# A MoE kernel's second part: pairs of blocks by turns with shared or with routed experts first

## The chip, the cores and the metric

One core of a Trainium2 chip runs the kernel; nothing else runs on the chip. The metric is the time of one execution on the device in microseconds (us); the time of the kernel before is the median of its executions.

## What is computed

Tokens x are 32 samples of 128 tokens of 128 features. Two layers of the same shape are applied, x = x + ffn(cond(x)) twice. In the first, cond is a mixture of 4 experts chosen 2 per sample, and ffn one of 8 experts that all run. The change lies in the second layer:

```
def _L1_cond_ref(x, t_emb, W_router, router_bias, s_w1, s_w3, s_w2, r_w1, r_w2):
    ...
    for e in range(N_SHARED):                      # 2 shared experts
        h = jax.nn.silu(x_flat @ s_w1[e].T) * (x_flat @ s_w3[e].T)
        shared_out = shared_out + h @ s_w2[e].T
    ...
    s = jax.nn.sigmoid((router_in @ W_router.T).astype(jnp.float32))
    _, topk_idx = jax.lax.top_k(s + router_bias, 2)
    ...                                            # gates: s of the two chosen, over their sum
    for e in range(N_EXPERTS):                     # 8 routed experts
        h = jax.nn.gelu(x_flat @ r_w1[e].T, approximate=False)
        routed_out = routed_out + h @ r_w2[e].T * gates_full[:, e:e + 1]
    out = (shared_out + routed_out) / (N_SHARED + TOP_K)

def _L1_ffn_ref(x, U1, V1, b1, U2, V2, b2):        # low rank, 32
    P = x @ U1;  H = jax.nn.gelu(P @ V1 + b1);  Q = H @ U2
    return Q @ V2 + b2
```

## The kernel before

The 4096 tokens are 8 blocks of 512 columns (NBLK, BLK), features on the 128 partitions. Work is a list of items, made by plan(): A and G are the first layer's mixture, B its ffn, and the second layer has S (shared expert, 4 items a block), R (routed expert, 8 items a block, one per expert) and F (final low-rank layer, 4 items a block). An item's number in the list is its slot; every engine's program is a loop over the slots, so the list orders all of them.

An item goes through the engines like this. TensorE's up() makes its columns in one of four PSUM banks (NZ, zb), three matmuls for each result since every fp32 number is split in a high and a low part (XHL; the weights WCH, WCL). S has two results, R and F one, and F's up is one matmul. ScalarE applies Silu (S, line 999), Gelu (R, line 995) or the tanh Gelu (F, line 992), each from another function table, so that an ACT_TABLE_LOAD stands where the kind changes. VectorE multiplies into Hf: for S the second result (line 1442), for R the token's gate for this expert (line 1449). Then the result is split again: HH, the high part, on ScalarE (line 1005) or VectorE (1459), HL, the rest, on VectorE (1462) or GpSimd (1542). The assignment is by kind: for R, HH is VectorE's for one item in four and HL is VectorE's for one in four; for S, HL is VectorE's but for blocks 2 and 3, where GpSimd has it. Five slots behind the up (LAG) comes down(), two matmuls from HH and HL (lines 897, 899) that add to one of two PSUM banks (ob), which a block holds from its first S or R item to its last.

The gates lie in the tile CWB, in 8 places of 128 x 512, one per expert; SyncE loads a place from the scratch tensor in HBM, a row spread over 128 partitions, 256 KB, for the next block as soon as the block before has multiplied by it (gate_slots, line 617). The gates themselves come from the choice, which is made twice: choose(0, .) for blocks 0 to 3 and choose(1, .) for blocks 4 to 7. Each is a sigmoid on ScalarE (line 959), some two dozen small VectorE operations spread over ten slots (pick; lines 1258 to 1310), a transposition on TensorE (line 808) and a write to scratch by SyncE.

When a block's S and R items are all down, low_rank (lines 965 and 1419) makes PS, from which F's ups start; behind F come read_q (970, 1427), last_mm (823) and add_y (1434), and the output leaves.

The order of the second part: for each pair of blocks b, b+1 the 8 S items, then F of the pair before, then the 16 R items. F of block 4 stands in the last pair, F of 5, 6 and 7 at the end (LATE).

Of the kernel before, what the change touches and what calls it, by code (L numbers as in the profile page):

```python
# [23 lines left out]
NO = 2  # L24
# [101 lines left out]
def build(nc, x_d, small_d, pack_d, wa_d, wb_d, wc_d, wf_d, scr_d, wup_d, wdown_d, out_d):  # L126
    with ExitStack() as ctx:
# [125 lines left out]
        def done(kind, blk, ex, f):  # L253
            return pos[kind, blk, ex, f].d
# [4 lines left out]
        t_c = [done("R", b, 7, 0) for b in range(NBLK)]  # L259
# [14 lines left out]
        for t, g in soft_a.items():  # L274
            for step, slot in ((0, 0), (2, 2), (3, 2), (4, 3), (5, 3)) if g == 0 else ((0, 0), (2, 2), (3, 3), (4, 4), (5, 5)):
# [4 lines left out]
                [pos["S", 2, 0, 0].k + i for i in (0, 1, 2, 3, 4, 5, 6, 7, 9, 10)]]  # L280
# [548 lines left out]
        def up(e, it):  # L829
            for j, z in enumerate(it.z):  # L830
# [12 lines left out]
                fresh = it.f == 0 and j == 0 and it.ex == 0  # L843
# [17 lines left out]
                if fresh and it.kind == "S":  # L861
                    e.wait_ge(s_b_hi, it.blk + 1)
# [17 lines left out]
                if fresh and it.kind == "S":  # L880
                    e.wait_ge(s_b_lo, it.blk + 1)
# [39 lines left out]
        def scalar_program(e):  # L921
# [11 lines left out]
            for k in range(slots):  # L933
# [26 lines left out]
                if k in low_rank:  # L960
                    b = low_rank[k]
                    e.wait_ge(s_down, pos["R", b, 7, 0].n + 1)
                    if ph_free(("P", b)):
                        e.wait_ge(*ph_free(("P", b)))
                    e.activation(PH[:, :], ob[pos["R", b, 7, 0].u % NO][:, :], ACT.Copy).then_inc(s_ph, 1)
# [46 lines left out]
        def vector_program(e):  # L1012
# [336 lines left out]
            for k in range(slots):  # L1349
# [303 lines left out]
```

## Time and profile before

| | us |
|---|---|
| median of 3 runs | 901.16 |
| lowest and highest | 900.01, 903.05 |
| the profiled execution | 900.65 |
| its span, first to last instruction | 898.9 |
| TensorE busy | 875.0 |
| VectorE busy | 683.0 |
| ScalarE busy | 576.9 |
| GpSimd busy | 408.7 |

The time has 1.75 us around the span. The granted TensorE clock is 0.997 of full speed over the span. Matmuls are pipelined, so that TensorE's busy time covers short stalls; its starts tell more. The second layer's part runs from about 725 us to the end.

### The profile page before, as it was taken

Reading aid. Unit: us, or ns where it says so; the run is one execution under the profiler, and the core shown is the slowest. Engines: PE = TensorE matmul, PEld = TensorE weight load, DVE = VectorE, ACT = ScalarE, POOL = GpSimd, SP = SyncE. Lnnn points to the kernel's source line nnn. Section 1 sums busy time; section 2 is a strip of 40 time slices with the busy share of each in tenths; the row PEclk is TensorE's granted clock in tenths of the full one; section 3 lists DMA queues with packets and bytes.
Section 4 is the critical chain, followed back from the end, with each engine's and each line's share of the span. In section 5 each row is a group of like instructions: output and inputs, shape, how many; then the busy total and the mean of one; then the engine's idle time right before and its main releaser. Section 6 shows DMA issues by size and latency. Waiting matters only on the chain.

```text
span 898.9 us, 12685 instructions
## 1 busy us (share of the span) xinstructions
PE 875.0 (97%) x3878; PEld 694.6 (77%) x3878; DVE 683.0 (76%) x1097; ACT 576.9 (64%) x1032; POOL 408.7 (45%) x378
## 2 busy tenths in 40 slices
PE   8899999999999999999999999999999998999996
PEld 5778788878888888888888888888888785777773
DVE  7667777878789786686686686686666876998887
ACT  7788788765555455555555555555555677989896
POOL 7447865035256352252253253253222226755465
PEclk9999999999999999999999999999999999999999
DMA  9588882023023112012012012011010069182640
GB/s 311 195 251 273 297 285 100 1 85 132 13 82 109 36 47 82 1 47 82 1 48 82 1 48 82 1 47 48 7 42 1 0 107 175 39 179 52 159 106 35
DMA packets 35828, 82.96 MB, mean 92 GB/s; under 512 B 4400, under 2 KB 14256, under 8 KB 33840
## 3 DMA queue, kind: packets, MB, share of 16 engines
q1 hardware_dynamic: 35760, 82.15, 30.8%
q8 instruction: 31, 0.51, 0.3%
q14 instruction: 37, 0.30, 0.1%
HBM read 71.13 MB, written 6.83 MB: 87 GB/s over the span
## 4 chain that ended last, share of the span: by engine, by line
PE 77%; DVE 8%; issue 4%; ACT 3%; DMA 3%; SPq 2%; POOL 2%; POOLq 0%; DVEq 0%; ACTq 0%
PE ps L863 17%; PE ps L882 16%; PE ps L868 16%; PE ps L917 8%; PE ps L919 8%; PE ps L912 8%; DMA CWB<-scratch 2%; DVE HL L1462 2%; PE ps L899 1%; PE ps L897 1%; ACT HH L1005 1%; DVE HH L1459 1%; POOL HL L1542 1%; DVE Hf L1449 1%; SPq L722 1%
## 5 line engine op out<-in xcount | busy, mean ns | idle before, releaser
L999 ACT ACTIVATE Sg<-ps 128x512 f32<-128x512 f32 x288 | 171.8, 598 | 246.2 <-PE ps L882 245.8
L1442 DVE TENSOR_TENSOR Hf<-ps,Sg 128x512 f32<-128x512 f32 x288 | 198.0, 688 | 149.1 <-ACT Sg L999 93.2
L1542 POOL TENSOR_TENSOR HL<-Hf,HH 128x512 fp32r<-128x512 f32 x136 | 182.3, 1347 | 172.4 <-ACT HH L1005 154.6
L1005 ACT ACTIVATE HH<-Hf 128x512 fp32r<-128x512 f32 x346 | 216.2, 625 | 24.9 <-DVE Hf L1442 12.9
L1462 DVE TENSOR_TENSOR HL<-Hf,HH 128x512 fp32r<-128x512 f32 x242 | 214.7, 887 | 4.2 <-ACT HH L1005 3.2
L863 PE MATMUL ps<-XHL,WBH 128*128 128x512 f32 x512 | 203.7, 398 | 1.2 <-DVE Hf L1442 1.2
L882 PE MATMUL ps<-XHL,WBH 128*128 128x512 f32 x512 | 202.1, 395 | 0.0
L868 PE MATMUL ps<-XHL,WBL 128*128 128x512 f32 x512 | 202.0, 395 | 0.0
L1557 POOL TENSOR_TENSOR XT<-XT,TMP 128x512 f32<-128x512 f32 x64 | 84.2, 1316 | 251.5 <-DVE TMP L1338 251.5
L863 PEld LDWEIGHTS ps<-XHL,WBH 128*128 128x128 f32 x512 | 96.1, 188 | 25.1 <-DVE Hf L1442 2.3
L882 PEld LDWEIGHTS ps<-XHL,WBH 128*128 128x128 f32 x512 | 96.0, 188 | 23.1
L868 PEld LDWEIGHTS ps<-XHL,WBL 128*128 128x128 f32 x512 | 96.2, 188 | 21.8
L1462 DVE TENSOR_TENSOR HL<-ps,HH 128x512 fp32r<-128x512 f32 (+1 forms) x122 | 73.7, 618 | 37.6 <-ACT HH L1005 36.4
L917 PE MATMUL ps<-HH,WBL 128*128 128x512 f32 x256 | 101.1, 395 | 0.0
L912 PE MATMUL ps<-HH,WBH 128*128 128x512 f32 x256 | 100.8, 394 | 0.0
L919 PE MATMUL ps<-HL,WBH 128*128 128x512 f32 x256 | 100.7, 393 | 0.0
L992 ACT ACTIVATE ps<-ps,GWU 128x512 f32<-128x512 f32 (+1 forms) x84 | 48.8, 585 | 17.8 <-PE ps L882 17.4
L917 PEld LDWEIGHTS ps<-HH,WBL 128*128 128x128 f32 x256 | 48.0, 188 | 11.9
L912 PEld LDWEIGHTS ps<-HH,WBH 128*128 128x128 f32 x256 | 48.0, 187 | 11.9 <-DVE TMP L1338 0.3
L919 PEld LDWEIGHTS ps<-HL,WBH 128*128 128x128 f32 x256 | 48.1, 188 | 11.2
L863 PE MATMUL ps<-XHL,WCH 128*128 128x512 f32 x128 | 51.9, 405 | 3.7 <-DVE Hf L1449 2.4
L1449 DVE TENSOR_TENSOR Hf<-ps,CWB 128x512 f32<-128x512 f32 x64 | 42.8, 682 | 10.4 <-ACT ps L995 7.9
(254 smaller groups left out, 1347.3 us busy)
## 6 DMA issues: line engine op xcount, KB each, us to landing
CWB<-scratch SPq DMA_DIRECT2D x68, 256.0 KB, 7.9
CWB<-scratch SPq DMA_DIRECT2D x15, 1024.0 KB, 4.7
GWD<-expert_down SPq DMA_DIRECT2D x21, 576.5 KB, 4.6
GWU<-expert_up SPq DMA_DIRECT2D x21, 514.0 KB, 5.1
ST<-in_wb_dram SPq DMA_DIRECT2D x8, 768.0 KB, 6.3
GX<-XT SPq DMA_DIRECT2D x68, 64.0 KB, 2.8
XT<-in_x_dram SPq DMA_DIRECT2D x8, 256.0 KB, 5.3
expert_up<-GWU SPq DMA_DIRECT2D x4, 512.0 KB, 3.8
```

What stands on the lines that cost most here:

```text
L863: e.matmul(o, wh, tokens(it, 0), start=True, stop=False)
L868: e.matmul(o, wl, tokens(it, 0), start=False, stop=False)
L882: e.matmul(o, wh, tokens(it, 1), start=False, stop=True).then_inc(s_z, 1)
L912: e.matmul(bk[:, 0:n], wh, HH[:, hs, 0:n], start=it.new, stop=False)
L917: e.matmul(bk[:, 0:n], wl, HH[:, hs, 0:n], start=False, stop=False)
L919: e.matmul(bk[:, 0:n], wh, HL[:, hs, 0:n], start=False, stop=it.last).then_inc(s_down, 1)
L999: e.activation(Sg[:, it.n % NG, :], zb[z % NZ][:, :], ACT.Silu).then_inc(s_act, 1)
L1005: e.activation(HH[:, it.n % NH, 0:it.cols], hidden_place(it), ACT.Copy).then_inc(s_hi_act, 1)
L1442: e.tensor_tensor(Hf[:, it.n % NS, :], zb[z % NZ][:, :], Sg[:, it.n % NG, :], ALU.mult).then_inc(s_prod, 1)
L1462: e.tensor_tensor(l, f, h.bitcast(F32), ALU.subtract).then_inc(s_lo_dve, 1)
L1542: e.tensor_tensor(HL[:, it.n % NH, :], Hf[:, it.n % NS, :], HH[:, it.n % NH, :].bitcast(F32), ALU.subtract).then_inc(s_lo_pool, 1)
L1557: e.tensor_tensor(XT[:, it.blk, :], XT[:, it.blk, :], TMP[:, t % 2, :], ALU.add).then_inc(s_acc, 1)
```

## The change

For pairs 0 and 2 (blocks 0, 1, 4, 5) S comes first and R last, for pairs 1 and 3 (blocks 2, 3, 6, 7) R first and S last. F of the pair before stands between the two in every pair, as it did. The mark of a block's last item is set where the list ends it, R for the one kind of pair and S for the other, and what went by R's eighth item (t_c, the bank, the semaphore's count) goes by that item. TensorE's waits for a block's tokens are at the block's first item, S or R. The second choice starts at the same slot as before, 24 items behind the second part's start, where R2 stands now and S2 stood.

```
 S0 S1 R0 R1  S2 S3 F0 F1 R2 R3  S4 S5 F2 F3 R4 R5  S6 S7 F4 R6 R7  F5 F6 F7   before
 S0 S1 R0 R1  R2 R3 F0 F1 S2 S3  S4 S5 F2 F3 R4 R5  R6 R7 F4 S6 S7  F5 F6 F7   after
```

```
--- before.py
+++ after.py
@@ -103,17 +103,21 @@
         return [Item("S", blk, f // 2, f % 2, False) for f in range(4)]
 
     def routed(blk):
-        return [Item("R", blk, e, 0, e == 7) for e in range(8)]
+        return [Item("R", blk, e, 0, False) for e in range(8)]
 
     def final(blk):
         return [Item("F", blk, 0, f, f == 3) for f in range(4)]
 
+
     for b in range(0, NBLK, 2):
-        items += shared(b) + shared(b + 1)
+        one, two = (shared, routed) if b % 4 == 0 else (routed, shared)
+        items += one(b) + one(b + 1)
         for f in (b - 2, b - 1):
             if 0 <= f < LATE:
                 items += final(f)
-        items += routed(b) + routed(b + 1)
+        for c in (b, b + 1):
+            items += two(c)
+            items[-1].last = True
     for b in range(LATE, NBLK):
         items += final(b)
     return items
@@ -256,7 +260,8 @@
         t_g = done("G", NGRP - 1, 0, 3)
         t_a = [max(t_g, done("A", b, 0, 3)) for b in range(NBLK)]
         t_b = [done("B", b, 7, 3) for b in range(NBLK)]
-        t_c = [done("R", b, 7, 0) for b in range(NBLK)]
+        end_c = [next(it for it in real if it.kind in "SR" and it.blk == b and it.last) for b in range(NBLK)]
+        t_c = [it.d for it in end_c]
         t_f = [done("F", b, 0, 3) for b in range(NBLK)]
 
         def when(times, after=0):
@@ -277,7 +282,7 @@
         exp_a = {t + 1: g for t, g in soft_a.items()}
 
         pick = [[lag_b[3] + 1 + i for i in (0, 1, 2, 3, 5, 6, 7, 8, 10, 11)],
-                [pos["S", 2, 0, 0].k + i for i in (0, 1, 2, 3, 4, 5, 6, 7, 9, 10)]]
+                [pos["R", 2, 0, 0].k + i for i in (0, 1, 2, 3, 4, 5, 6, 7, 9, 10)]]
         pick_at = {}
         for g in range(2):
             for i, t in enumerate(pick[g]):
@@ -840,7 +845,7 @@
                     continue
                 o = zb[z % NZ][:, 0:it.cols]
                 wh, wl = up_weights(it, j)
-                fresh = it.f == 0 and j == 0 and it.ex == 0
+                fresh = it.new and j == 0 if it.kind in "SR" else it.f == 0 and j == 0 and it.ex == 0
                 if it.kind == "A" and it.blk == 0 and it.f == 0:
                     e.wait_ge(s_wa_hi, 1)
                 if it.kind == "G" and it.f == 0:
@@ -858,7 +863,7 @@
                         e.wait_ge(s_x_end, 2 * it.blk - 11)
                 if fresh and it.kind == "B":
                     e.wait_ge(s_a_hi, it.blk + 1)
-                if fresh and it.kind == "S":
+                if fresh and it.kind in "SR":
                     e.wait_ge(s_b_hi, it.blk + 1)
                 e.matmul(o, wh, tokens(it, 0), start=True, stop=False)
                 if it.kind == "A" and it.blk == 0 and it.f == 0:
@@ -877,7 +882,7 @@
                     e.wait_ge(s_g_lo, it.blk + 1)
                 if fresh and it.kind == "B":
                     e.wait_ge(s_a_lo, it.blk + 1)
-                if fresh and it.kind == "S":
+                if fresh and it.kind in "SR":
                     e.wait_ge(s_b_lo, it.blk + 1)
                 e.matmul(o, wh, tokens(it, 1), start=False, stop=True).then_inc(s_z, 1)
 
@@ -959,10 +964,10 @@
                     e.activation(pick_place(g)[0], LR[:, 16 * g:16 * g + 16, 0:8], ACT.Sigmoid).then_inc(s_exp, 1)
                 if k in low_rank:
                     b = low_rank[k]
-                    e.wait_ge(s_down, pos["R", b, 7, 0].n + 1)
+                    e.wait_ge(s_down, end_c[b].n + 1)
                     if ph_free(("P", b)):
                         e.wait_ge(*ph_free(("P", b)))
-                    e.activation(PH[:, :], ob[pos["R", b, 7, 0].u % NO][:, :], ACT.Copy).then_inc(s_ph, 1)
+                    e.activation(PH[:, :], ob[end_c[b].u % NO][:, :], ACT.Copy).then_inc(s_ph, 1)
                 if k in read_q:
                     b = read_q[k]
                     e.wait_ge(s_down, pos["F", b, 0, 3].n + 1)
@@ -1417,7 +1422,7 @@
                     if b >= 2:
                         e.wait_ge(s_z, pos["F", b - 2, 0, 3].z[0] + 1)
                     e.scalar_tensor_tensor(out=PS[:, b % 2, :], in0=PH[:, :].bitcast(F32), scalar=col("m2"),
-                                           in1=ob[pos["R", b, 7, 0].u % NO][:, :], op0=ALU.mult,
+                                           in1=ob[end_c[b].u % NO][:, :], op0=ALU.mult,
                                            op1=ALU.add).then_inc(s_ps, 1)
                 if k in read_q:
                     b = read_q[k]
```

VectorE, from the last multiplications of R1 to the second choice's first six operations, first before, then after (the number behind L is the line; in the changed kernel lines are 5 higher):

```order
L1449 TENSOR_TENSOR Hf<-ps,CWB 128x512
L1442 TENSOR_TENSOR Hf<-ps,Sg 128x512
L1459 CAST HH<-Hf 128x512
L1258 TENSOR_TENSOR ps<-ps,sm 128x128
L1260 TENSOR_REDUCE r<-ps 128x16
L1262 TENSOR_TENSOR ps<-ps,r 128x128
L1442 TENSOR_TENSOR Hf<-ps,Sg 128x512
L1265 TENSOR_TENSOR ps<-ps,sm 128x128
L1267 TENSOR_REDUCE r<-ps 128x16
L1269 TENSOR_TENSOR q<-ps,r 128x128
L1442 TENSOR_TENSOR Hf<-ps,Sg 128x512
```

```order
L1454 TENSOR_TENSOR Hf<-ps,CWB 128x512 x2
L1464 CAST HH<-Hf 128x512
L1263 TENSOR_TENSOR ps<-ps,sm 128x128
L1265 TENSOR_REDUCE r<-ps 128x16
L1267 TENSOR_TENSOR ps<-ps,r 128x128
L1454 TENSOR_TENSOR Hf<-ps,CWB 128x512
L1270 TENSOR_TENSOR ps<-ps,sm 128x128
L1272 TENSOR_REDUCE r<-ps 128x16
L1274 TENSOR_TENSOR q<-ps,r 128x128
L1454 TENSOR_TENSOR Hf<-ps,CWB 128x512
L1467 TENSOR_TENSOR HL<-Hf,HH 128x512
```

The eight S multiplications (L1442) beside the choice's small operations give place to R's (L1454), with VectorE's HL (L1467) and HH (L1464) of R between them. The low-rank operation of block 1, which stands behind the fourth step in both, isn't shown.

ScalarE at the same place, before and after:

```order
L995 ACTIVATE ps<-ps 128x512
L1005 ACTIVATE HH<-Hf 128x512
L959 ACT_TABLE_LOAD
L959 ACTIVATE ps<-LR 128x128
L999 ACT_TABLE_LOAD
L999 ACTIVATE Sg<-ps 128x512 x2
L1005 ACTIVATE HH<-Hf 128x512
L999 ACTIVATE Sg<-ps 128x512
```

```order
L1000 ACTIVATE ps<-ps 128x512
L1010 ACTIVATE HH<-Hf 128x512
L964 ACT_TABLE_LOAD
L964 ACTIVATE ps<-LR 128x128
L1000 ACT_TABLE_LOAD
L1000 ACTIVATE ps<-ps 128x512 x2
L1010 ACTIVATE HH<-Hf 128x512
L1000 ACTIVATE ps<-ps 128x512
```

The sigmoid stays between two table loads; the second loads R's table where it loaded S's.

SyncE, from the write of the first choice to the end, before and after:

```order
L684 DMA scratch<-q 128x128
L617 DMA CWB<-scratch 128x512 x24
L684 DMA scratch<-q 128x128
L617 DMA CWB<-scratch 128x512 x6
L699 DMA out_dram<-CB 128x512
L617 DMA CWB<-scratch 128x512 x4
L699 DMA out_dram<-CB 128x512
L617 DMA CWB<-scratch 128x512 x12
L699 DMA out_dram<-CB 128x512
```

```order
L689 DMA scratch<-q 128x128
L622 DMA CWB<-scratch 128x512 x32
L689 DMA scratch<-q 128x128
L622 DMA CWB<-scratch 128x512 x8
L704 DMA out_dram<-CB 128x512 x2
L622 DMA CWB<-scratch 128x512 x6
L704 DMA out_dram<-CB 128x512
L622 DMA CWB<-scratch 128x512 x4
L704 DMA out_dram<-CB 128x512
```

Loads of gates (L617, now L622) come 32 in a row instead of 24 ahead of the second choice's write (L684, now L689), and the outputs of blocks 0 and 1 (L699, now L704) leave behind the loads for block 4 instead of among those for block 3 and block 4.

## Rows read from the trace of the kernel before

**Rows 1.** The page's first part: busy us, share of the span, instructions.

```profile
PE 875.0 (97%) x3878; PEld 694.6 (77%) x3878; DVE 683.0 (76%) x1097; ACT 576.9 (64%) x1032; POOL 408.7 (45%) x378
```

**Rows 2.** Windows: PE, PEld, DVE, ACT, POOL busy us, TensorE clock, DMA share, GB/s.

```profile
731.70:754.60 22.90, 20.88 (x85) 15.19 (x84) 15.20 (x26) 16.15 (x30) 12.80 (x10) 1.00 0.99 178
754.60:780.00 25.40, 22.90 (x95) 16.95 (x94) 20.90 (x44) 22.15 (x35) 17.69 (x13) 1.00 0.36 62
780.00:798.40 18.40, 18.40 (x79) 13.96 (x77) 17.74 (x28) 16.53 (x32) 14.60 (x12) 1.00 0.83 185
798.40:822.30 23.90, 22.30 (x92) 16.61 (x91) 19.69 (x29) 20.73 (x33) 6.88 (x5) 1.00 0.33 58
822.30:840.40 18.10, 18.10 (x80) 14.66 (x79) 17.79 (x29) 16.20 (x32) 14.78 (x12) 1.00 0.76 179
...
860.30:878.10 17.80, 17.40 (x72) 12.66 (x71) 16.89 (x25) 15.92 (x32) 14.56 (x12) 1.00 0.54 134
878.10:898.90 20.80, 12.83 (x44) 7.13 (x42) 15.90 (x25) 11.96 (x20) 10.21 (x8) 0.95 0.10 38
```

**Rows 3.** The tile CWB, 725.7 to 758.3: ns min/median/max, first and last start us.

```profile
L617 SPq DMA_DIRECT2D CWB<-scratch x24: 320/1412/1844, 725.7 to 756.6; - x24
L1449 DVE TENSOR_TENSOR Hf<-ps,CWB x16: 678/692/693, 731.7 to 754.6; 128x512 f32<-128x512 f32 x16
...
DMA to landing us min/median/max: 3.8/9.9/11.3
```

**Rows 4.** VectorE's timeline: start us, us, engine, line, operation, tiles, idle before.

```profile
735.60 0.69 DVE L1449 TENSOR_TENSOR Hf<-ps,CWB 128x512 f32<-128x512 f32 x1 [0.26 <-DMA CWB<-scratch]
...
753.18 0.69 DVE L1449 TENSOR_TENSOR Hf<-ps,CWB 128x512 f32<-128x512 f32 x1 [0.38 <-issue]
```

**Rows 5.** The chain of waits, 741 to 756 us: start, us, what.

```profile
743.07 9.74 DMA CWB<-scratch
```

**Rows 6.** ScalarE's timeline at the second choice's sigmoid.

```profile
754.55 1.28 ACT L959 ACT_TABLE_LOAD   x1
...
756.15 1.28 ACT L999 ACT_TABLE_LOAD   x1
757.44 1.09 ACT L999 ACTIVATE Sg<-ps 128x512 f32<-128x512 f32 x2
```

**Rows 7.** VectorE's timeline, steps of the second choice.

```profile
758.68 0.42 DVE L1459 CAST HH<-Hf 128x512 fp32r<-128x512 f32 x1
759.01 0.29 DVE L1258 TENSOR_TENSOR ps<-ps,sm 128x128 f32<-128x128 f32 x1
...
759.87 0.68 DVE L1442 TENSOR_TENSOR Hf<-ps,Sg 128x512 f32<-128x512 f32 x1
760.47 0.29 DVE L1265 TENSOR_TENSOR ps<-ps,sm 128x128 f32<-128x128 f32 x1
...
768.11 1.18 DVE L1301 TENSOR_SCALAR r<-r 128x16 f32<-128x16 f32 x1
```

**Rows 8.** Line 1442: S multiplications of blocks 2-3, 4-5 and 6-7.

```profile
L1442 DVE TENSOR_TENSOR Hf<-ps,Sg x8: 666/680/692, 758.1 to 770.1; 128x512 f32<-128x512 f32 x8
...
L1442 DVE TENSOR_TENSOR Hf<-ps,Sg x8: 676/687/692, 800.2 to 811.4; 128x512 f32<-128x512 f32 x8
...
L1442 DVE TENSOR_TENSOR Hf<-ps,Sg x8: 679/688/692, 842.1 to 853.3; 128x512 f32<-128x512 f32 x8
```

**Rows 9.** TensorE's timeline, one S item.

```profile
725.63 0.39 PE L863 MATMUL ps<-XHL,WCH 128*128 128x512 f32 x1
...
727.48 0.39 PE L863 MATMUL ps<-XHL,WCH 128*128 128x512 f32 x1
```

**Rows 10.** The tile CWB, 822.2 to 841, blocks 4 and 5.

```profile
L1449 DVE TENSOR_TENSOR Hf<-ps,CWB x16: 673/677/692, 822.3 to 840.4; 128x512 f32<-128x512 f32 x16
L617 SPq DMA_DIRECT2D CWB<-scratch x15: 319/320/1837, 823.0 to 839.1; - x15
...
DMA to landing us min/median/max: 3.0/6.7/10.7
```

More of the change, by code:

```diff
@@ L105, in routed @@
     def routed(blk):
-        return [Item("R", blk, e, 0, e == 7) for e in range(8)]
+        return [Item("R", blk, e, 0, False) for e in range(8)]
     def final(blk):
@@ L111, in plan @@
     for b in range(0, NBLK, 2):
-        items += shared(b) + shared(b + 1)
+        one, two = (shared, routed) if b % 4 == 0 else (routed, shared)
+        items += one(b) + one(b + 1)
         for f in (b - 2, b - 1):
@@ L115, in plan @@
                 items += final(f)
-        items += routed(b) + routed(b + 1)
+        for c in (b, b + 1):
+            items += two(c)
+            items[-1].last = True
     for b in range(LATE, NBLK):
@@ L258, in build @@
         t_b = [done("B", b, 7, 3) for b in range(NBLK)]
-        t_c = [done("R", b, 7, 0) for b in range(NBLK)]
+        end_c = [next(it for it in real if it.kind in "SR" and it.blk == b and it.last) for b in range(NBLK)]
+        t_c = [it.d for it in end_c]
         t_f = [done("F", b, 0, 3) for b in range(NBLK)]
@@ L279, in build @@
         pick = [[lag_b[3] + 1 + i for i in (0, 1, 2, 3, 5, 6, 7, 8, 10, 11)],
-                [pos["S", 2, 0, 0].k + i for i in (0, 1, 2, 3, 4, 5, 6, 7, 9, 10)]]
+                [pos["R", 2, 0, 0].k + i for i in (0, 1, 2, 3, 4, 5, 6, 7, 9, 10)]]
         pick_at = {}
@@ L842, in up @@
                 wh, wl = up_weights(it, j)
-                fresh = it.f == 0 and j == 0 and it.ex == 0
+                fresh = it.new and j == 0 if it.kind in "SR" else it.f == 0 and j == 0 and it.ex == 0
                 if it.kind == "A" and it.blk == 0 and it.f == 0:
@@ L860, in up @@
                     e.wait_ge(s_a_hi, it.blk + 1)
-                if fresh and it.kind == "S":
+                if fresh and it.kind in "SR":
                     e.wait_ge(s_b_hi, it.blk + 1)
@@ L879, in up @@
                     e.wait_ge(s_a_lo, it.blk + 1)
-                if fresh and it.kind == "S":
+                if fresh and it.kind in "SR":
                     e.wait_ge(s_b_lo, it.blk + 1)
@@ L961, in scalar_program @@
                     b = low_rank[k]
[L962 removed]
+                    e.wait_ge(s_down, end_c[b].n + 1)
                     if ph_free(("P", b)):
                         e.wait_ge(*ph_free(("P", b)))
[L965 removed]
+                    e.activation(PH[:, :], ob[end_c[b].u % NO][:, :], ACT.Copy).then_inc(s_ph, 1)
                 if k in read_q:
```

2 lines of the change are left out of this document (1 added, 1 removed).

## The prediction

> **What bounds the kernel now.** I read the page's first part, then the second part of the program stretch by stretch (the windows), then the one tile that the new order uses more densely (CWB, the gates), then the timelines of VectorE and ScalarE around the choice. S2 is the shared experts of block 2, R2 its routed experts (R2.0 to R2.7, one item each), F2 its final layer; blocks count from 0, so the third block is block 2.
>
> TensorE is busy 97% of the span [rows 1], so a gain must come from where it waits. Up to the routed experts of blocks 0 and 1 both programs have the same instructions in the same order on every engine; the change lies after 731.7 us, in the last 167 us. There it is busy 18.4 of 18.4 us beside R2 and R3 and 18.1 of 18.1 beside R4 and R5, but 20.9 of 22.9 beside R0 and R1, 22.9 of 25.4 beside S2, S3, F0, F1, and 12.8 of 20.8 in the tail [rows 2]. So two pairs of routed blocks run without a loss and one pair does not, with the same arithmetic in each. The DMA column tells them apart: 0.99 beside R0 and R1, 0.83 and 0.76 beside the others. Every routed item multiplies by a gate row that was spread over 128 partitions, 256 KB, and there are 8 places for such rows, one per expert. The place is loaded again only after the block before has used it. R0 and R1 run back to back on loads that have just begun: 24 loads follow each other, 9.9 us from issue to landing in the median and up to 11.3, and even the issue takes SyncE 1.4 us in the median against 0.32 at the least [rows 3]. VectorE is released by such a load at 735.60 (R0.3) and, by the chain of waits, again at 753.18 (R1.6) [rows 4, 5]. Between them lie 11 loads: 17.58 / 11 = 1.60 us for a load, while an item needs about 1.2 us of the compute engines (18.1 us from first to last of 16, over 15 intervals). R2 to R5 escape this because in the order of before every second block's loads arrive during 24 items of S and F.
>
> **What the change does to that, part by part.** I count on VectorE's clock: the start of the multiplication that ends each stage, since TensorE, which runs at most four results ahead of it, ends up behind the same event.
>
> *R0 and R1*: unchanged, last multiplication at 754.6.
>
> *R2 and R3 now follow at once.* Their 16 loads are not hidden any more. R3.7 is 17 loads behind R1.6: 753.18 + 17 x 1.60 = 780.4. Against this stands what VectorE has to do. The sigmoid of the second choice stays between two table loads of 1.28 us [rows 6], so R2.0 is multiplied at 758.1 as S2.0 is now. The choice took 12.0 us from 758.1 to 770.1 beside eight S multiplications [rows 7, 8]: three dependent steps of 0.33 us a slot (759.01 to 759.87) and one slot with a step of 1.18 us. In those slots of before GpSimd computes HL for S; for R VectorE has two of the eight HL (0.6 us from start to start) and two HH (0.34) besides, so R2.7 comes at 770.1 + 1.2 + 0.3 = 771.6. Eight more items at 0.9 (VectorE alone: 0.6 for the multiplication, a quarter of 0.6 and of 0.34, and the copy) to 1.16 us (five matmuls of 0.232 [rows 9]) end between 778.8 and 780.9. Loads and choice thus end about together; neither is added to the other, since the loads already queued go on landing while VectorE chooses. I take 780.2 for R3.7. Bounds: 778.7, if a load takes 1.50; 784, if the choice's delay also delays the reissue of loads by its full 4 us.
>
> *F0 and F1* then cost what they cost behind S3 now: from S3's last multiplication at 770.1 to R2.0 at 780.0, 9.9 us [rows 2, 8], two table loads in it either way: 790.1.
>
> *S2 to S5 in a row.* Sixteen items, 15 intervals. One S item is eight matmuls, 725.63 to 727.48 = 1.85 us [rows 9], and TensorE is the slowest engine there. Eight of them took 11.2 us instead of 7 x 1.85 = 13.0, since TensorE enters ahead; that 1.8 is had once: 15 x 1.85 - 1.8 = 26.0, so 816.1. The outputs of F0 and F1 move from R2 and R3 to here, where VectorE has room; I cost them at nothing, and 0.7 us each if they hadn't.
>
> *F2 and F3*: as now, 811.4 to 822.3 = 10.9 [rows 2, 8]: R4.0 at 827.0.
>
> *R4 to R7 in a row.* R4's loads are long in. R5's first load is issued 0.7 us after R4.0's multiplication (823.0 against 822.3) and lands 3.0 later, then latency climbs to 10.7 because loads at 1.6 follow items at 1.2 [rows 10]. With two blocks in a row the climb ends before it hurts; with four, 24 loads queue: 0.7 + 3.0 + 23 x 1.60 = 40.5 us from R4.0 to R7.7, against 18.1 + 1.2 + 17.8 = 37.1 when the loads are in time. So 867.5.
>
> *F4*, now behind R7: as now behind S7, 853.3 to 860.3 = 7.0: 874.5. *S6 and S7*: 11.2: 885.7. *The tail*, F5 to F7 with the outputs: 898.9 - 878.1 = 20.8: 906.5.
>
> *What goes.* Sigmoid to S2, R3 to S4 and R5 to S6 are three joins that vanish, F to S and R to F come in their place; the table loads of the second part fall, by the two programs' order, from 12 to 10, 2 x 1.28 = 2.6 us of ScalarE. This is already in the sum, since I went from stage to stage; ScalarE is at 16.2 to 16.5 of 18.1 to 18.4 us beside R and not the bound [rows 2].
>
> Sum: 906.5 - 898.9 = +7.6 us. The profiled execution took 900.65, so 908.2 for its like; the median of the runs is 901.16, 0.5 above, so **908.8**.
>
> Two rules would have it otherwise. The Trainium skill, ScalarE: Activation LUTs, Table sets: the hidden batching unit and the rules behind it, says to do all work of one table set before switching, at about 2.66 us for each switch (What ACT_TABLE_LOAD costs); that speaks for the change and would make its two fewer switches worth 5.3 us. The trace has 1.28 us for a load, and the next activation starts 0.02 us behind it [rows 6]. The Trainium skill, DMA: Bandwidth & Descriptors, Anatomy of one DMA, fits a transfer at 2.0 us plus its bytes over 436e3 (for transfers issued by GpSimd), which is an estimate of 0.6 us a load for 256 KB when several overlap; then no routed item would ever wait for a gate. The trace has 1.60, with all 16 DMA engines at a share of 0.99.
>
> **The rivals.**
>
> *A. The sum above*: gates bound eight blocks' worth in two long runs. For it: the two pairs of before differ in nothing but the state of the loads.
>
> *B. The loads keep up, and fewer switches pay.* If the 1.60 were not a rate of the DMA engines but came from the start (R0's eight loads issued at once) then loads at the pace of the items would land in time. R3.7 would come at 754.6 + 3.5 (sigmoid) + 18.4 = 776.5 or so, 3.7 earlier, and R4 to R7 would take 37.1, 3.4 less: +0.5 us; with one table load of 1.28 and the join R3 to S4 (1.8 us from 798.4 to 800.2, of which 0.6 is the wait of the table) gained, 900 to 902. It decides if a load lands faster than one in 1.2 us. For it: bytes moved are only 178 GB/s. Against it: the share of 0.99, and that beside R4 and R5, issued one by one, latency climbs from 3.0 to 10.7 as well.
>
> *C. The choice does not fit beside R2.* TensorE has to transpose the choice's result two slots behind it, in front of its own item, and all that is queued behind (the ups of R3, the downs of R2) waits for VectorE. If VectorE's extra work in these slots (about 7 us of choice, 12.0 less eight times 0.6) is paid after the loads instead of under them, R3.7 comes at 784: 912.6.
>
> *D. A load takes 1.50.* In the two drains the last loads may come closer. Then R0 to R3 end 1.5 earlier, R4 to R7 2.3 earlier, and the F stretches behind R, whose table load needn't wait for an HH of ScalarE, are each 0.4 shorter: 904.2.
>
> **How the numbers follow.** A 0.52, D 0.22, C 0.12, B 0.14. A measurement here tells 0.3% (2.7 us) from nothing. A, C and D are slower than 903.9, D in most of its width; B is half faster, half the same. Slower 0.84, same 0.09, faster 0.07. The range 903.5 to 912.5 leaves out B and half of C.
>
> **What would show it.** The multiplications by gates: 32 in a row with R3.7 near 780, DMA share near 1.0 from 731 to 780 and from about 840 to 867, TensorE waiting for VectorE's L1454 (L1449 now) and VectorE for the landing of CWB in R2, R3 and R7. S2 to S5 at 1.85 us an item without a wait. No wait for CWB in R2 and a DMA share under 0.9 would mean B; VectorE busy without a gap from 758 to 780 with loads landed well before use would mean C. I am wrong if R4 to R7 take 37 us.

## The result, and the profile after

The changed kernel takes 912.46 us (median of 4 runs, 911.04 to 914.89), against 901.07 for the kernel before beside it. The ratio is 1.0129 [1.0114, 1.0143], 11.6 us of 901. The forecast was 908.8, range 903.5 to 912.5: slower, as said, but 11.6 us where 7.6 were forecast. By the ratio on 901.16 us the time is 912.8 (901.16 x 1.0129), just above the range. The profiled execution took 912.01 us with a span of 910.2. VectorE's multiplication by a gate is L1454, that of an S item L1447, TensorE's transposition of the choice L813, the choice's last step L1312.

The first part of the page of the changed kernel, as [rows 1]:

```profile
PE 878.5 (97%) x3878; PEld 697.4 (77%) x3878; DVE 682.9 (75%) x1097; ACT 574.6 (63%) x1030; POOL 407.4 (45%) x378
```

Work is the same on every engine but ScalarE, which has two instructions less. So the 11.6 us are waiting, and work at a lower clock. The windows show where; columns as in [rows 2] (busy us of PE, PEld, DVE, ACT, POOL, then clock, DMA share, GB/s). In order: R0 and R1; R2 and R3; F0 and F1; S2 to S5; F2 and F3; R4 and R5; R6 and R7 with their start; F4 with S6 and S7; the tail.

```profile
731.30:753.80 22.50, 20.89 (x85) 15.21 (x85) 15.03 (x26) 15.91 (x29) 12.80 (x10) 1.00 1.02 182
753.80:783.30 29.50, 21.75 (x77) 15.77 (x76) 21.26 (x51) 19.16 (x34) 15.41 (x13) 0.88 0.81 145
783.30:794.20 10.90, 9.24 (x36) 6.06 (x35) 9.77 (x12) 9.47 (x15) 6.50 (x5) 1.00 0.69 135
794.20:820.70 26.50, 26.50 (x116) 21.42 (x116) 18.00 (x27) 18.98 (x35) 11.59 (x9) 1.00 0.06 21
820.70:831.60 10.90, 9.71 (x39) 6.70 (x38) 9.13 (x11) 10.83 (x17) 4.35 (x3) 1.00 0.01 2
831.60:849.70 18.10, 18.10 (x80) 14.71 (x79) 17.78 (x29) 16.23 (x32) 14.66 (x12) 1.00 0.78 183
849.70:871.00 21.30, 19.66 (x80) 14.15 (x79) 16.31 (x27) 15.97 (x30) 16.04 (x13) 1.00 0.77 165
871.00:888.00 17.00, 16.80 (x71) 12.55 (x70) 14.70 (x22) 14.06 (x24) 5.43 (x4) 1.00 0.01 1
888.00:910.20 22.20, 14.18 (x52) 8.73 (x50) 16.52 (x27) 13.40 (x23) 7.69 (x6) 0.91 0.13 47
```

Two rows matter. Beside R2 and R3, TensorE works 21.75 of 29.5 us and its granted clock is 0.88; in [rows 2] no pair of R takes over 22.9 and every window in front of the tail has a clock of 1.00. Beside R6 and R7 it works 19.66 of 21.3 us, where a pair with its loads in time is busy 18.1 of 18.1.

Put against the terms of the prediction, from one last multiplication on VectorE to the next (us):

| stretch | predicted | after | off |
|---|---|---|---|
| start to R1.7 | 754.6 | 753.8 | -0.8 |
| R1.7 to R3.7 | 25.6 | 29.5 | +3.9 |
| F0, F1, to S2.0 | 9.9 | 10.9 | +1.0 |
| S2 to S5 | 26.0 | 26.5 | +0.5 |
| F2, F3, to R4.0 | 10.9 | 10.9 | 0 |
| R4 to R7 | 40.5 | 39.3 | -1.2 |
| F4, to S6.0 | 7.0 | 6.0 | -1.0 |
| S6, S7 | 11.2 | 11.1 | -0.1 |
| tail | 20.8 | 22.2 | +1.4 |

The sum is 910.2 instead of 906.5. One stretch carries the miss, R1.7 to R3.7. The first row is no finding: up to R1.7 the programs are the same, and the traces with 256 KB loads have R1.7 anywhere from 753.2 to 754.8. VectorE's timeline there, at R2.3, at the end of the choice with R2.7, and at R3.7 (start, us, line, operation, idle time before):

```profile
764.53 0.69 DVE L1454 TENSOR_TENSOR Hf<-ps,CWB 128x512 f32<-128x512 f32 x1 [1.66 <-DMA CWB<-scratch]
...
771.92 0.37 DVE L1312 TENSOR_TENSOR q<-ps,q 128x128 f32<-128x128 f32 x1
772.15 1.26 DVE L1454 TENSOR_TENSOR Hf<-ps,CWB 128x512 f32<-128x512 f32 x2
...
783.27 0.68 DVE L1454 TENSOR_TENSOR Hf<-ps,CWB 128x512 f32<-128x512 f32 x1
```

And TensorE's:

```profile
768.44 0.50 PE L904 MATMUL ps<-HL,WD 128*128 128x512 f32 x1 [0.52 <-POOL HL L1547]
...
772.44 0.30 PE L813 MATMUL ps<-sm,q 128*128 128x128 f32 x1 [3.50 <-DVE q L1312]
772.50 0.48 PE L868 MATMUL ps<-XHL,WCH 128*128 128x512 f32 x1
...
773.35 0.63 PE L902 MATMUL ps<-HH,WD 128*128 128x512 f32 x1
773.77 0.63 PE L904 MATMUL ps<-HL,WD 128*128 128x512 f32 x1
774.20 0.63 PE L868 MATMUL ps<-XHL,WCH 128*128 128x512 f32 x1
```

VectorE waits for a gate once, 1.66 us at R2.3, and never again up to R3.7. TensorE instead stands for 3.50 us in front of the transposition L813, which needs the choice's last step. Behind it in its queue are the ups of R3 and the downs of R2, and they come in a burst when it ends. From 773.35 on matmuls start 0.42 to 0.43 us apart, where [rows 9] has 0.23 (1.85 us for eight). Three short windows of the same columns, the last two inside slow spells, the first in front of one:

```profile
753.80:758.00 4.20, 2.38 (x11) 1.58 (x9) 1.21 (x3) 4.08 (x6) 1.30 (x1) 1.00 1.08 154
...
760.00:762.00 2.00, 2.00 (x5) 1.61 (x6) 1.93 (x6) 1.66 (x4) 1.11 (x1) 0.50 0.69 128
...
774.00:776.00 2.00, 2.00 (x6) 1.52 (x6) 0.89 (x2) 0.99 (x3) 2.00 (x2) 0.50 1.00 175
```

A clock of 0.50 is the lower of TensorE's two levels, 1.2 instead of 2.4 GHz. It is granted twice, 759.5 to 762.9 and 773.2 to 776.6, 3.4 us each. Ahead of the first TensorE was busy 2.38 of 4.2 us (the join around the sigmoid of the second choice), ahead of the second it did nothing from 770 to 772 (the transposition). What decides between the levels is not shown: the same 4.2 us behind R1.7 in the kernel before have TensorE busy 2.54 us, and its clock stays at 1.00 there, and behind it too [rows 2]:

```profile
754.60:758.80 4.20, 2.54 (x10) 1.34 (x8) 1.43 (x4) 3.89 (x6) 1.28 (x1) 1.00 1.02 163
```

By an estimate, half of 6.8 us, 3.4 us of matmul time, is lost if TensorE is the bound throughout.

The loads of that stretch (tile CWB, 725 to 758; columns of [rows 3]):

```profile
L622 SPq DMA_DIRECT2D CWB<-scratch x24: 320/1441/1836, 725.1 to 755.5; - x24
...
DMA to landing us min/median/max: 3.8/10.6/14.6
```

They are those of [rows 3] but for one that took 14.6 us, the one R2.3 waited for. While it was under way, a 16 KB packet of the queue that brings instructions took 6.1 us; no packet of such a queue took over 2.4 us in the other traces. R2.7 came 18.3 us behind R1.7 here, and 16.3 and 16.4 us in two kernels below without a late load (no reload; the transposition later). So some 2 us of R2 in this execution belong to one load. The median of the runs is no lower than this execution, though; where the other executions lost as much isn't shown. A kernel below that turns only blocks 2 and 3 has the same program up to here and no late load in its trace: its R1.7 to R3.7 is 27.9 us.

### The profile page after: what moved, and what is told of

Its sections match the earlier page's. It is cut to its first block, busy times and chain, and to the rows that moved or that the text cites. A ratio compares the mean times of both kernels' runs of the same rounds, so it can differ in the third digit from the quotient of the medians.

```text
span 910.2 us, 12683 instructions
## 1 busy us (share of the span) xinstructions
PE 878.5 (97%) x3878; PEld 697.4 (77%) x3878; DVE 682.9 (75%) x1097; ACT 574.6 (63%) x1030; POOL 407.4 (45%) x378
## 4 chain that ended last, share of the span: by engine, by line
PE 75%; DVE 8%; DMA 7%; issue 4%; ACT 3%; SPq 2%; POOL 1%; POOLq 0%; DVEq 0%; ACTq 0%
PE ps L868 16%; PE ps L887 16%; PE ps L873 16%; PE ps L922 8%; PE ps L924 8%; PE ps L917 8%; DMA CWB<-scratch 6%; DVE HL L1467 2%; PE ps L904 1%; ACT HH L1010 1%; PE ps L902 1%; DVE HH L1464 1%; DVE Hf L1454 1%; PE ps L790 1%; DMA XT<-in_x_dram 1%
## 5 line engine op out<-in xcount | busy, mean ns | idle before, releaser
L1447 DVE TENSOR_TENSOR Hf<-ps,Sg 128x512 f32<-128x512 f32 x288 | 198.1, 689 | 150.3 <-ACT Sg L1004 88.7
L1467 DVE TENSOR_TENSOR HL<-Hf,HH 128x512 fp32r<-128x512 f32 x242 | 211.2, 873 | 4.0 <-ACT HH L1010 3.2
L873 PEld LDWEIGHTS ps<-XHL,WBL 128*128 128x128 f32 x512 | 96.2, 188 | 21.7
L1467 DVE TENSOR_TENSOR HL<-ps,HH 128x512 fp32r<-128x512 f32 (+1 forms) x122 | 73.7, 618 | 36.4 <-ACT HH L1010 35.3
L1454 DVE TENSOR_TENSOR Hf<-ps,CWB 128x512 f32<-128x512 f32 x64 | 43.4, 685 | 21.7 <-ACT ps L1000 10.9
L922 PEld LDWEIGHTS ps<-HH,WBL 128*128 128x128 f32 x256 | 48.0, 188 | 11.8
L924 PEld LDWEIGHTS ps<-HL,WBH 128*128 128x128 f32 x256 | 48.1, 188 | 11.2
```

Source lines behind the costliest of these rows:

```text
L873: e.matmul(o, wl, tokens(it, 0), start=False, stop=False)
L922: e.matmul(bk[:, 0:n], wl, HH[:, hs, 0:n], start=False, stop=False)
L924: e.matmul(bk[:, 0:n], wh, HL[:, hs, 0:n], start=False, stop=it.last).then_inc(s_down, 1)
L1447: e.tensor_tensor(Hf[:, it.n % NS, :], zb[z % NZ][:, :], Sg[:, it.n % NG, :], ALU.mult).then_inc(s_prod, 1)
L1467: e.tensor_tensor(l, f, h.bitcast(F32), ALU.subtract).then_inc(s_lo_dve, 1)
```

## The experiments

All results are ratios to the kernel before, run beside each kernel, with a 95% interval; it ran at 899.8 to 900.3 us there, about 1 us below the 901.07 above, so a time in us compares with one of the first runs only after that 1 us. Stages are from one trace of each kernel, on VectorE's multiplications, as in the table. A *join* is the time from the last multiplication of one stretch to the first of the next. For comparison, in the kernel before: R0 to R1 22.9, S2 to S3 12.0, R2 to R3 18.4, R4 to R5 18.1, tail 20.8.

### The choice back beside S2

```
-                [pos["R", 2, 0, 0].k + i for i in (0, 1, 2, 3, 4, 5, 6, 7, 9, 10)]]
+                [pos["S", 2, 0, 0].k + i for i in (0, 1, 2, 3, 4, 5, 6, 7, 9, 10)]]
...
         def pick_place(g):
-            if g:
-                return [v(ab_bank("pick")[:, i * 128:i * 128 + 128]) for i in range(3)]
             return v(q2[:, 0:128]), v(q2[:, 128:256]), v(q3[:, 128:256])
```

> The changed order, with the second choice begun 24 items later, beside S2 instead of R2, its three intermediate arrays in SBUF (as the first choice has them) instead of a PSUM bank. In the changed kernel the multiplications went from R1.7 to R3.7 in 29.5 us, with TensorE waiting 3.8 us for the choice's result ahead of its transposition, and the clock granted at half twice for 3.4 us. Theory 1 (the choice beside R2 is what made this stretch longer than the loads' 25.6): it falls to 25 to 26, the half clock is gone, and S2, S3 take it without a loss; 907.5 to 909.5 us in all. Theory 2 (the loads alone bound the stretch, and the late load of R2.3 of that one execution did the rest): 911.5 to 913, and the stretch stays above 28.

Measured 912.42, 1.0141 [1.0122, 1.0160], where neither theory holds as written: the stretch fell below what the first said, and the whole didn't fall at all. R1.7 to R3.7 fell from 29.5 to 22.3 (join 0.6, R2 and R3 21.7) with no wait in front of a transposition and no half clock there. But F0, F1 to S2.0 came to 12.6, and S2 and S3 took 18.1 instead of 12.0. The window of S2 and S3, and VectorE and GpSimd in it:

```profile
789.30:807.40 18.10, 14.29 (x57) 10.27 (x57) 17.62 (x34) 9.84 (x18) 10.47 (x8) 1.00 0.04 16
```

```profile
789.86 1.40 DVE L1257 TENSOR_TENSOR q<-q,sm 128x128 f32<-128x128 f32 x1
791.29 0.29 DVE L1259 TENSOR_REDUCE r<-q 128x16 f32<-128x128 f32 x1
791.62 1.11 DVE L1261 TENSOR_TENSOR q<-q,r 128x128 f32<-128x128 f32 x1
```

```profile
789.81 1.30 POOL L1541 TENSOR_TENSOR HL<-Hf,HH 128x512 fp32r<-128x512 f32 x1 [3.34 <-ACT HH L1004]
791.31 1.27 POOL L1541 TENSOR_TENSOR HL<-Hf,HH 128x512 fp32r<-128x512 f32 x1 [0.20 <-ACT HH L1004]
```

The edit did more than move the choice. It had no PSUM bank there, so its arrays lie in SBUF, and a step that takes 0.29 us with an operand in PSUM [rows 7] takes 1.40 while GpSimd runs its 1.30 us subtraction, and 1.11 beside the next. The Trainium skill, SBUF — State Buffer, SBUF: two separate sides, has the rule: a port pair is shared by VectorE and GpSimd as an exclusive lock, taken for a whole instruction, and a VectorE operation with two SBUF inputs needs it against a GpSimd operation that reads SBUF. By that rule, the trace agrees: the 1.40 us step ends just behind GpSimd's instruction, the reduction with one input is at 0.29. So this run shows that R1.7 to R3.7 is 7.2 us shorter without the choice beside it, some 2 of them by the late load, but not what the move would bring in all.

### No loads of gates after the first block of a half

```
-            for ex in range(8):
+            for ex in range(8 if b % 4 == 0 else 0):
...
-                    e.wait_ge(f_gate[it.ex], 16 * (it.blk + 1))
+                    e.wait_ge(f_gate[it.ex], 16 * (it.blk // 4 + 1))
```

> The changed kernel without the reloads of gates: blocks 1 to 3 multiply by block 0's gates, 5 to 7 by block 4's, so 16 loads of 256 KB are left of 64. Theory 1 (choice bounds R2 and R3, loads bound R0, R1 and R4 to R7): R0 and R1 take 19 to 20 instead of 22.6 us, R4 to R7 37 instead of 39.3, R2 and R3 still 27 to 28 instead of 29.5; 905 to 907.5 us. Theory 2 (loads bound all of it): R2 and R3 fall to about 22, and the whole to 899 to 902.

The same on the kernel before:

> The kernel before without the reloads of gates (blocks 1 to 3 multiply by block 0's, 5 to 7 by block 4's). Only R0 and R1 wait for loads in it: their 22.9 us fall to 19 or 20, and the whole to 897 to 898.5. The difference to the changed kernel without reloads is then what order and choice cost without any load.

| | ratio | R0 to R1 | R1.7 to R3.7 | R6 to R7 |
|---|---|---|---|---|
| after | 1.0129 | 22.5 | 29.5 | 21.3 with its join |
| after, no reload | 1.0057 [1.0040, 1.0074] | 19.1 | 28.1 | 18.8 with its join |
| before, no reload | 0.9968 [0.9957, 0.9979] | 19.1 | | |

The first theory holds for the changed kernel (905.21 us), and the second run is within what it expected once it is put on 901 us (898.2). The loads cost the new order 1.0129 - 1.0057 = 0.0072, 6.5 us, and the old one 2.9. But R2 and R3, the stretch that I had bound by loads, gain 1.4 us of their 29.5 when the loads are gone. The waits of the run without them, its multiplications, and its window of half clock:

```profile
PE ps L813 <- DVE q L1312: 3.5, 1, 3.5
```

```profile
L1454 DVE TENSOR_TENSOR Hf<-ps,CWB x16: 672/680/692, 754.0 to 778.8; 128x512 f32<-128x512 f32 x16
```

```profile
765.40:772.20 6.80, 4.99 (x13) 3.96 (x14) 4.38 (x12) 3.42 (x7) 3.84 (x3) 0.50 0.04 11
```

The wait of 3.5 us at the transposition is there with no reload at all, and so is the half clock, 6.8 us in one piece. Here it is not granted behind the join R1 to R2 but from 765.1 on, while TensorE still stands in front of the transposition.

### No second choice, with and without the loads

The second choice is left out, and blocks 4 to 7 are gated by the first one's scratch. Three kernels: after without the choice; after without choice and reloads; before without both.

```
-        for g in range(2):
+        for g in range(1):
             for i, t in enumerate(pick[g]):
...
-                    e.wait_ge(f_scr[1][b // 4], 16)
-                    src = scr_d[1, b // 4].rearrange("(e t) k -> e (t k)", e=8)[ex][
+                    e.wait_ge(f_scr[1][0], 16)
+                    src = scr_d[1, 0].rearrange("(e t) k -> e (t k)", e=8)[ex][
```

> The changed kernel without the second choice (no sigmoid, no choice on VectorE, no transposition): blocks 4 to 7 multiply by the gates of blocks 0 to 3, loaded as before. By the stages seen: R1 to R3.7 at the loads' pace, 22 to 23 us instead of 29.5, the rest as in the changed kernel: 904 to 906 us. That would put the choice's cost in this order at 6 to 8 us. If the choice cost only the wait at the transposition (3.5 us), it is 908 to 909.

> The changed order without the second choice and without reloads of gates (blocks 1 to 7 multiply by block 0's gates, loaded twice). What is left is the order of S, R and F. Stages: 19.6 + 0.6 + 18.2 for R0 to R3, 10.9, 26.5 for S2 to S5, 10.9, 36.9, 6.0, 11.1, 22.2: 895 to 897 us.

> The kernel before without the second choice and without reloads, as the mate of the last one. Kernel before without reloads is 897.0; the join R1 to S2 falls from 3.4 to 1.8 and S2, S3 from 12.0 to 11.1: 893 to 895 us. If order alone is neutral, both are level; by my stages this one is 1.5 to 2.5 us faster, from the tail behind R7 (20.7) against S7 (22.2) and the join R3 to F0 (10.9 against 9.9).

Measured 904.46, 1.0042 [1.0026, 1.0059]; 896.56, 0.9960 [0.9946, 0.9975]; and 894.75, 0.9934 [0.9918, 0.9951]: all three within 1 us of what was expected. With the runs above this makes a table of four for R1.7 to R3.7 in the new order:

| | no loads | loads |
|---|---|---|
| no choice | 18.9 | 22.1 |
| choice | 28.1 | 29.5 |

Loads alone, from the kernel after without the choice (tile CWB, then the window):

```profile
L1452 DVE TENSOR_TENSOR Hf<-ps,CWB x17: 683/691/693, 753.6 to 775.7; 128x512 f32<-128x512 f32 x17
...
DMA to landing us min/median/max: 5.2/9.5/10.7
```

```profile
753.60:775.70 22.10, 20.07 (x78) 13.53 (x77) 15.40 (x27) 15.56 (x30) 15.36 (x12) 1.00 1.01 197
...
762.00:765.00 3.00, 2.51 (x11) 1.60 (x10) 2.31 (x5) 2.23 (x5) 2.26 (x2) 1.00 0.97 305
```

That is a stretch bound by loads: DMA share 1.01, 16 intervals in 22.1 us, so 1.38 us a load. It isn't the 1.60 of the run from R0.3 to R1.6. Nor is it an even pace: the landings of the stretch are 0.6 to 2.4 us apart, and in the 3 us of the second row 305 GB/s move at nearly the same DMA share. So a load had no fixed price here, and 1.60 and 1.38 are averages.

With the choice the stretch is 29.5, and loads add 1.4 to 28.1 instead of 3.2 to 18.9, with the late load among the 1.4. In the trace without a late load (only blocks 2 and 3 turned, below) it is 27.9 with all its loads, no longer than without any: they do hide under the choice.

With the two orders each run with both, without loads and without either, the parts of the whole have a price (as a share of the kernel before's time, and in us):

| | old order | new order | difference |
|---|---|---|---|
| neither | 0.9934 | 0.9960 | 0.0026, 2.3 us |
| choice adds | 0.0034 | 0.0097 | 0.0063, 5.7 us |
| loads add to that | 0.0032 | 0.0072 | 0.0040, 3.6 us |

The sum of the differences is 11.6 us, as it must be; each difference is good to 2 or 3 us, since each ratio has an interval of 0.001 to 0.002 to either side. So about half of the loss is the choice beside R2. The order alone, without either, also loses: every one of its 5 runs (896.35 to 898.20) is above the 4 of the old order (894.18 to 895.57). About 1.5 us of it is the tail, 22.2 against 20.8 in their traces.

### The transposition four slots later

```
-                [pos["R", 2, 0, 0].k + i for i in (0, 1, 2, 3, 4, 5, 6, 7, 9, 10)]]
+                [pos["R", 2, 0, 0].k + i for i in (0, 1, 2, 3, 4, 5, 6, 7, 13, 14)]]
```

> The changed kernel with the second choice's transposition on TensorE four items later (R3.5 instead of R3.1), and the copy behind it. It takes the in-order wait in front of R3.1 away and leaves the choice's work on VectorE where it is. If that wait (3.8 us of TensorE, and the half clock after it) is on the path: R2.7 to R3.7 falls from 11.1 to 8 or 9 us and the whole to 909 to 910.5. If VectorE itself is the bound there: no change, 912 to 913.

Measured 908.94, 1.0098 [1.0081, 1.0115]. No instruction is removed; TensorE's transposition only stands four items further back, and the copy of its result with it. Its wait is gone, so is the second spell of half clock, and R1.7 to R3.7 is 25.8 (join 3.5, then 22.3) instead of 29.5, of which some 2 us are the late load. R2.7 to R3.7 takes 9.4 instead of 11.1 (11.8 without reloads). Of the whole this is worth 1.0129 - 1.0098 = 0.0031, 3 us, good to 2. The multiplications and the window:

```profile
L1454 DVE TENSOR_TENSOR Hf<-ps,CWB x16: 670/680/692, 758.3 to 780.6; 128x512 f32<-128x512 f32 x16
```

```profile
758.30:781.00 22.70, 19.23 (x70) 13.49 (x70) 21.91 (x49) 15.70 (x29) 15.31 (x12) 0.92 0.58 133
```

VectorE is busy 21.91 of 22.70 us: this is the case that I had forecast, where VectorE's work sets the end, and the stretch takes the 25.6 us of the forecast to 0.2. One spell of half clock is left, 3.4 us at 760.4.

### One pair at a time

The rule of the order with one pair turned, blocks 2 and 3 or blocks 6 and 7 (the latter with the choice beside S2, where the old order has it):

```
-        one, two = (shared, routed) if b % 4 == 0 else (routed, shared)
+        one, two = (shared, routed) if b != 2 else (routed, shared)
```

> One half of the change: only blocks 2 and 3 have R first (R2 R3 F0 F1 S2 S3), blocks 6 and 7 have S first as before. By the stages of both traces, added up, this half has 9.3 of the 11.3 us: 909.5 to 911. If the two halves depend on each other (ScalarE's two fewer table loads, the outputs), it would differ from 901.1 + 9.3 by over 2 us.

> The other half of the change: only blocks 6 and 7 have R first (R6 R7 F4 S6 S7), blocks 2 and 3 have S first and the second choice stands beside S2 as before. By the stages: R4 to R7 39.3 us instead of 18.1 + 17.8 and the joins between, F4 and tail: +2.0 us, so 902.5 to 904. If the loads cost nothing in it, it ends at 900 to 901.5.

Measured 908.77, 1.0104 [1.0087, 1.0121] and 902.09, 1.0020 [1.0009, 1.0031]; 9.4 and 1.8 us, 11.2 together of 11.6, so within the noise of some 2 us the two pairs don't act on each other. Turning blocks 6 and 7 gives R6 and R7 at 20.7 (join 0.6) and the longer tail of 22.2; turning blocks 2 and 3 leaves the tail at 20.8. The trace of the kernel with only blocks 2 and 3 turned shows R2 and R3 beside the choice a second time. R1.7 to R3.7, the half clock behind the transposition, and the wait in front of it:

```profile
753.20:781.10 27.90, 21.44 (x77) 16.15 (x76) 21.07 (x51) 19.33 (x34) 15.45 (x13) 0.88 0.74 163
770.30:773.70 3.40, 3.40 (x9) 2.72 (x10) 2.12 (x5) 1.11 (x2) 2.02 (x3) 0.50 0.46 142
...
PE ps L813 <- DVE q L1312: 3.5, 1, 3.5
```

VectorE waits for no load in it, and R2.7 to R3.7 is 11.1 us again.

### No reload, and the choice beside S2

The two edits of the first two experiments together.

> The changed order, without the reloads of gates (blocks 1 to 3 multiply by block 0's, 5 to 7 by block 4's) and with the second choice beside S2. If loads and choice are all that makes the changed order slower, it is level with the kernel before without reloads: 896 to 899. If the stages R3 to F0 and the tail behind S7 cost by themselves (10.9 instead of 9.9 and 22.2 instead of 20.8 us), it is 1 to 3 us above that kernel.

Measured 903.07, 1.0037 [1.0023, 1.0050], where I had expected 896 to 899. R2 and R3 took 18.2 us, as hoped, but with the choice in SBUF S2 and S3 took 18.0, and the join of F0 and F1 12.5. The expectation had the choice beside S2 at the old order's price, which was measured with its arrays in PSUM. The new order with the choice beside S2 and in PSUM was not run.

### Gates of two blocks in one load

Each load brings the gates of a pair of blocks, 512 KB with rows of 4 KB, in places that ST and WBH0 leave free by then:

```
-        for b in range(NBLK):
+        for b in range(0, NBLK, 2):
...
-                        (b % 4) * BLK:(b % 4) * BLK + BLK].partition_broadcast(P)
-                    e.dma_start(gate_place(ex), src).then_inc(f_gate[ex], 16)
+                        (b % 4) * BLK:(b % 4) * BLK + 2 * BLK].partition_broadcast(P)
+                    e.dma_start(gate_pair(ex), src).then_inc(f_gate[ex], 16)
```

> The kernel before with gates loaded for two blocks at once: 32 loads of 512 KB with rows of 4 KB instead of 64 of 256 KB with rows of 2 KB, in CWB, the staging tile ST and the weight tile WBH0, all idle by then. R1 needs no reload behind R0. If a load's time goes by its rows' count (1.6 us for 128 rows of 2 KB; the 1 MB loads of 8 KB rows take 4.7 us to landing), 8 loads land in 13 to 20 us and R0 and R1 take 19 to 21 instead of 22.9: 897.5 to 899.5. If it goes by bytes alone (164 GB/s), R1's gates land at about 751 and R0's start later: 900 to 902.

> The changed kernel with both mends: gates loaded for two blocks at once (512 KB, rows of 4 KB) and the transposition four items later. R0 and R1 19.1 as in the kernel before with such loads, R2 and R3 22 (VectorE with the choice), R4 to R7 37: 902 to 904 us. If loads of 512 KB still run late for four blocks in a row, R2, R3 and R6, R7 stay at 22 to 24 and 20: 905 to 907.

On the kernel before: 897.07, 0.9965 [0.9953, 0.9977], less than the kernel before by 3 us and than the changed one by 15, and within the noise of the one that loads nothing again (0.9968). Its window of R0 and R1, and the loads of CWB on its page (KB each, median us from issue to landing):

```profile
731.10:750.20 19.10, 19.10 (x84) 15.47 (x83) 16.20 (x26) 16.05 (x30) 13.40 (x11) 1.00 0.79 252
```

```profile
CWB<-scratch SPq DMA_DIRECT2D x16, 512.0 KB, 7.4
```

R0 and R1 take 19.1 instead of 22.9 us; TensorE works in all of it. The first eight loads land 1.69 us apart on average (728.8 to 740.7), the first eight of half the size in the kernel before 1.75 (729.5 to 741.8), so the bytes were not what a load cost: 252 GB/s with a DMA share of 0.79, against 178 with 0.99 in [rows 2]. The edit also frees R1 of reloads behind R0; what longer rows and what the added places are worth each was not run apart.

On the kernel after, together with the later transposition: 903.23, 1.0028 [1.0017, 1.0038], so 9 of the 11.6 us are won back; the old order with the same loads is still 5.7 us ahead. R2 and R3, then R4 to R7:

```profile
755.60:777.90 22.30, 19.07 (x68) 13.37 (x69) 21.51 (x49) 15.32 (x29) 14.92 (x12) 0.92 0.18 57
...
826.20:863.20 37.00, 36.62 (x158) 29.09 (x157) 35.82 (x54) 31.80 (x61) 31.45 (x24) 1.00 0.40 128
```

R4 to R7 take 37.0, the 37.1 that the prediction gave for loads in time. R2 and R3 stay at 22.3 with the DMA engines nearly idle (0.18): with no load and no transposition in the way, VectorE's own work (21.51 of 22.30 busy) is the price of the choice there, 3.9 us over the 18.4 of the kernel before. One spell of half clock lies in it too (mean clock 0.92); what that costs by itself isn't shown.

## Where the prediction fell short, and what in it held

*The bound of R0 and R1* was read rightly. Without reloads they take 19.1 instead of 22.9 us, with loads of a pair of blocks 19.1 as well. The wait was for loads, and not for their bytes: twice the bytes a load came at the same pace.

*R1.7 to R3.7* was the step that failed, 25.6 against 29.5. Its form held in this: neither is added to the other (18.9, 22.1, 28.1, 29.5). But loads and choice don't end together, and the signs that I had named for loads as the bound weren't there: VectorE waited for CWB once in R2 and never in R3, and the DMA share was 0.81. Both sizes were wrong. The load side, 1.60 a load for 26 us, is 22.1 when loads stand alone. The choice side was allowed 24.2 to 26.3 us (R3.7 between 778.8 and 780.9) and takes 28.1. The part up to R2.7, 17.0, was near (16.3 and 16.4; 18.3 in the profiled execution with its late load). The sentence that fell is "eight more items at 0.9 to 1.16 us" for the way from R2.7 to R3.7. It took 11.1 us, or 1.39 an item. I had costed these items as if every engine went on working under the choice, and had put TensorE's wait in front of the transposition at nothing in the sum: the ups of R3 and the downs of R2 stood 3.5 us behind it, and then ran at half the clock for 3.4 us (5 us in the kernel without reloads, where the clock had fallen 2 us ahead of the transposition). With the transposition moved, the same eight items took 9.4, and the whole stretch 25.8. The wait and the half clock were removed together, so their shares stay open.

*Rival C* named this mechanism with its place, and its time, R3.7 at 784 and 912.6 us in all, is close to what was measured (783.3, 912.5). That its time came out so near is luck in part: the 7 us that it names would give 787, its 784 is the bound of the sum (the choice's full 4 us), and the late load is in the 783.3. Nor was its sign there: VectorE was busy 17.34 of 22 us from 758 to 780, with gaps. I had given it 0.12 since I priced it as work of VectorE paid after the loads, not as a wait of TensorE, and the trace of before had no stretch with a half clock ahead of the tail to price the rest. But the place was known: the transposition stands two slots behind the choice's last step and in front of TensorE's own item, and TensorE runs up to four results ahead of VectorE, so it had to arrive early there.

*F0 and F1* were 10.9, not 9.9. Without the choice the same stretch of the old order is 10.9 too (763.18 to 774.05 in that trace), so the 9.9 of before were short because of the choice: it had delayed the last multiplication of S3, and the stretch is counted from there. An interval carries the lateness of the stretch ahead of it.

*S2 to S5* (26.5 for 26.0), *F2 and F3*, *S6 and S7* held. *F4* took 6.0 for 7.0, in every kernel with blocks 6 and 7 turned, with loads and without; why wasn't looked into. The outputs of F0 and F1, costed at nothing, did cost next to nothing: TensorE is busy in all 26.5 us.

*R4 to R7* took 39.3 for 40.5. They are bound by loads at their end, as said, since without reloads they take 36.9 (18.1, then 18.8 with the join) and with pairs 37.0. The formula's 1.60 for each of 23 loads would have to be 1.55. In fact R4 and R5 went at the pace of the items (18.1), and R6 and R7 at 21.2 / 16 = 1.33 an item, with waits for CWB of 2.3 us in three places:

```profile
L1454 DVE TENSOR_TENSOR Hf<-ps,CWB x17: 674/691/692, 849.7 to 870.9; 128x512 f32<-128x512 f32 x17
...
  DMA CWB<-scratch: 2.3, 3
...
DMA to landing us min/median/max: 8.3/9.2/9.8
```

*The tail* was copied from the old order, 20.8, and took 22.2. In the old order the last items ahead of it are eight routed ones, now they are four shared ones, and TensorE waits once for a block's sum PS from VectorE, 1.04 us:

```profile
892.40 0.47 PE L843 MATMUL ps<-PS,V1S 128*128 128x512 f32 x1 [1.04 <-DVE PS L1424]
```

```profile
891.51 0.74 DVE L1424 SCALAR_TENSOR_TENSOR PS<-PH,sm,ps 128x512 fp32r<-128x512 f32 x1
```

The kernels with blocks 6 and 7 in the new order have 22.2, with them in the old order 20.7 or 20.8, whatever the choice and the loads do. So the order makes it; that this one wait is the whole of it isn't shown.

*The table loads*, 12 to 10: nothing in a stage shows a gain. The trace has fewer instructions on ScalarE and no shorter stretch for it, since ScalarE bounds none of the long ones.

*Rival B* is refuted in its total (the loads cost 6.5 us here, and the time is far from 900 to 902), though R2 did go nearly without a wait for CWB. *D*, a load at 1.50, is half right: loads go at 1.33 to 1.6 on average, but that lay beside the point in R2 and R3, where VectorE and TensorE under the choice set the end.

What stays open: why the loads from R0.3 to R1.6 go at 1.60 and later ones at 1.33 to 1.38, with some 0.6 apart among them, and why one load took 14.6 us. Neither was tried.

## What to carry to other kernels

When small dependent work moves beside denser work, don't only add its duration: find the instruction of the bound engine that needs its last result, and ask where in that engine's queue it stands. Here one 128x128 transposition, four slots too early, cost 3 us (good to 2).

When many equal loads from DRAM to all partitions bound a stretch, try fewer loads with longer rows before moving anything: half as many loads of twice the size, in places kept for two blocks, won 3 us in a kernel in which reordering lost 12.

## What the runs showed that I had not expected

- Two spells of TensorE at half clock (0.50 for 3.4 us each) in the middle of a kernel whose clock is otherwise 1.00 there; each came after a stretch in which TensorE was waiting (2.38 of 4.2 us busy; none of 2). Here the wait at the transposition was paid a second time in the clock; not every wait was, since 2.54 of 4.2 us busy in the kernel before left the clock at 1.00.
- Eight loads of 512 KB in rows of 4 KB land at the pace of eight of 256 KB in rows of 2 KB in the same place of the program, 1.69 us apart against 1.75.
- VectorE's steps of 0.29 us take 1.1 to 1.4 beside GpSimd's subtraction if both inputs lie in SBUF; with an operand in PSUM they stayed at 0.29 beside the same S items [rows 7].
